# A Mamba-style block on one core: the last pass's y laid down in row order, gates read back in two parts, and Pool's share of a convolution halved

## The reference, cut to what matters

```python
xi, z = split(x @ in_proj_w.T)                       # 192 channels each
xi = silu(depthwise_conv3x3(xi) + conv_b)
x_hwwh = stack([rows(xi), columns(xi)])              # two orders of the pixels
xs = concat([x_hwwh, flip(x_hwwh)])                  # four directions
# per direction: delta = softplus(dt), B, C from projections of xs; then the scan
h = exp(delta * A) * h + (delta * u) * B             # along L, for 16 states
y = sum_n(h * C) + D * u
# the columns' y is turned back to row order, and the four are added
y = y_rows + y_rows_flipped + turn(y_columns) + turn(y_columns_flipped)
y = layer_norm(y, on_g, on_b)                        # over the 192 channels
y = y * silu(z)                                      # the gates
out = y @ out_proj_w.T                               # 96 channels
x1 = inp * skip_scale + out;  x2n = layer_norm(x1, ln2_g, ln2_b)
```

## Time and profile before

| | |
|---|---|
| median of 3 runs | 13864.06 us (13862.24 to 13864.12) |
| the profiled execution | 13858.02 us, span 13856.2 us |
| mean granted TensorE clock | 0.894 of full speed |
| busy, share of the span | PE 78%, DVE 85%, Pool 75%, ACT 50% |

### The profile page before, as it was taken

How to read it: one execution, slowest core, us unless ns; L and a number is a source line. 1 busy time by engine, 2 the same in 40 slices (tenths; PEclk the granted TensorE clock), 3 DMA queues, 4 the chain that set the end, 5 groups by cost and what they waited for, 6 DMA issues and landing times. The chain is left out here.

```text
span 13856.2 us, 95545 instructions
## 1 busy us (share of the span) xinstructions
PE 10835.5 (78%) x24854; PEld 4165.7 (30%) x24854; DVE 11827.1 (85%) x8429; ACT 6948.7 (50%) x10308; POOL 10323.1 (75%) x4469
## 2 busy tenths in 40 slices
PE   6777877778777787877877778787787777877778
PEld 2333323333233332333322333233332323323333
DVE  6999579995799957999579995799957999579995
ACT  4454455554545445555455454554544545545455
POOL 5999359993599925999259992699926999269992
PEclk8999889999899997999889998899988999989998
DMA  4677346773467734677346773477734677347772
GB/s 136 215 219 215 94 128 214 221 213 91 135 213 221 214 85 137 214 220 214 83 138 215 219 215 80 140 217 218 216 78 141 215 219 215 77 148 215 219 215 72
DMA packets 765007, 2408.50 MB, mean 174 GB/s; under 512 B 205712, under 2 KB 207760, under 8 KB 752976
## 3 DMA queue, kind: packets, MB, share of 16 engines
q1 hardware_dynamic: 764400, 2401.78, 58.8%
HBM read 2300.18 MB, written 67.11 MB: 171 GB/s over the span
## 5 line engine op out<-in xcount | busy, mean ns | idle before, releaser
L1225 POOL TENSOR_TENSOR state<-state,c_sb 128x1024 f32<-128x1024 f32 x3072 | 7179.5, 2358 | 450.6 <-ACT carry L1052 448.7
L988 PE MATMUL ps<-state,wt 128*128 128x512 f32 x12288 | 6310.4, 656 | 144.2 <-ACT ya L1046 108.8
L988 PEld LDWEIGHTS ps<-state,wt 128*128 128x128 f32 x12288 | 2547.5, 211 | 3015.4 <-issue 2454.3
L1184 DVE TENSOR_TENSOR_SCAN state<-decay,carry,ps 128x1024 f32<-128x1024 f32 x1440 | 3379.5, 2347 | 86.2 <-DVE ps L1171 36.6
L1052 ACT COPY carry<-state 128x1 f32<-128x1 f32 x3072 | 586.2, 191 | 4870.7 <-DVE state L1184 4860.8
L965 PE MATMUL ps<-parts,sel 114*128 114x512 bf16 (+1 forms) x3840 | 1282.7, 419 | 2127.0 <-DVE state L1184 2125.6
L1214 POOL TENSOR_TENSOR dbu<-b_sb,du 128x1024 f32<-128x1024 f32 x1152 | 2717.1, 2359 | 231.9 <-DVE du L1199 231.9
L1171 DVE TENSOR_TENSOR ps<-ps,du 128x1024 f32<-128x1024 f32 x1920 | 2323.5, 1210 | 0.9
L1094 ACT ACTIVATE decay<-delta,a_neg 128x1024 f32<-128x1024 f32 x1920 | 2195.3, 1144 | 6.2
L1184 DVE TENSOR_TENSOR_SCAN state<-ps,carry,dbu 128x1024 f32<-128x1024 f32 x864 | 2013.4, 2330 | 4.1 <-POOL dbu L1214 4.1
L965 PEld LDWEIGHTS ps<-parts,sel 114*128 114x128 bf16 (+1 forms) x3840 | 259.8, 100 | 3678.3 <-DVE state L1184 3426.1
(11 more groups left out here) (208 smaller groups left out, 10860.9 us busy)
## 6 DMA issues: line engine op xcount, KB each, us to landing
c_sb<-bc SPq DMA_DIRECT2D x2048, 512.0 KB, 4.3
c_sb<-bc SPq DMA_DIRECT2D x2048, 256.0 KB, 5.5
b_sb<-bc SPq DMA_DIRECT2D x768, 512.0 KB, 4.6
b_sb<-bc SPq DMA_DIRECT2D x768, 256.0 KB, 5.4
x_nat<-x SPq DMA_DIRECT2D x17, 1536.0 KB, 9.2
gates<-gate_a SPq DMA_DIRECT2D x8, 2048.0 KB, 6.8
gate_a<-gates SPq DMA_DIRECT2D x8, 2048.0 KB, 8.8
x_tok<-x SPq DMA_DIRECT2D x288, 48.0 KB, 1.8
```

Source lines behind the costliest of these rows:

```text
L988: mm = pe.matmul(py[:, q * CH:(q + 1) * CH], col("ident"), state[:, slot(g, n), q * CH:(q + 1) * CH], start=(n == 0), stop=False)
L1184: dve.tensor_tensor_scan(state[:, slot(g, n), way], rate, what, 0.0 if fresh else carry[:, n:n + 1], ALU.mult, ALU.add)\
L1225: pool.tensor_tensor(state[:, slot(g, n), :], state[:, slot(g, n), :], c_sb[:, n % CRING, :], ALU.mult).then_inc(S["weighted"], 1)
```

## The change

Four edits:

1. `prep_b`: Pool's part of the remainder's convolution is 8 image rows (512 elements per partition) instead of 16. DVE does 8 more rows (`OWN_ROWS`) in the upper half of `conv_acc`, in nine taps behind its second group of taps of the a part. ACT takes `conv_acc` out when both are done.
2. `scan`: in the last pass `take_y` writes a new tile `y5`, in two copies: partitions 0 to 63 as they are, and partitions 64 to 127, which hold columns, into row order, reading PSUM with a step of 64 elements.
3. `post_a`: with `y5` in one order, `fold` is one matmul with a matrix `fold_w` (two identities side by side, twice), and the mean is taken of `ya` and `y5` themselves. It no longer waits for the folded copy, but `fold` of the next chunk waits until this one is centred. Pool adds the squares of the remainder to those of the a part, so that the variance needs one matmul. ACT's gain and offset go into DVE's instructions (`scalar_tensor_tensor`). The lags of the stages are shorter by one.
4. `post_a`: the gates and gn come back in two parts, the first two chunks and the other six, each with its own semaphore; the weights of the later part share the second one.

```diff
-POOL_ROWS = HH // 2
+POOL_ROWS = HH // 4
+OWN_ROWS = HH // 4
+FIRST = 2
...
+                nc.vector.tensor_tensor(fold_w[:, 0:DR], low, up, ALU.add)
+                nc.vector.tensor_tensor(fold_w[:, DR:128], low, up, ALU.add)
...
+                    act.wait_ge(S["conv_r"], 18)
+                    ur_out(conv_acc[:, :], 0, POOL_ROWS + OWN_ROWS).then_inc(S["ur_ready"], 1)
...
+                    def r_tap(t, before=0):
+                        if before:
+                            acc, first, last = rc(conv_acc[:, CH:SC]), POOL_ROWS, POOL_ROWS + OWN_ROWS
+                        else:
+                            acc, first, last = rc(ps2[2][:, :]), POOL_ROWS + OWN_ROWS, HH
...
-                    for i in range(1, NCH // SLOTS):
-                        a_taps(i)
+                    a_taps(1)
+                    for t in range(9):
+                        r_tap(t, 9)
+                    a_taps(2)
+                    a_taps(3)
...
-                        act.copy(chunk(yr if T % 3 == 2 else ya, T, at), like(py[:, :], T)).then_inc(S["y_taken"], 1)
+                        if T == 5:
+                            act.copy(y5[0:DR, span(at * SC, SC)], py[0:DR, :])
+                            by_row = y5[DR:128, :].rearrange("p (h w) -> p h w", w=W)
+                            last = act.copy(by_row[:, :, span(at * (SC // H), SC // H)],
+                                            py[DR:128, :].rearrange("p (w h) -> p h w", h=H))
...
+                    for part, here in ((slice(0, FIRST * CH), "back_first"), (slice(FIRST * CH, L), "back_in")):
+                        sp.dma_start(gate_a2[:, part], gate_dram[0:DA, part]).then_inc(S[here], 16)
+                        sp.dma_start(gate_r2[:, part], gate_dram[DA:DI, part]).then_inc(S[here], 16)
+                        sp.dma_start(gn_2[:, part], gn_dram[:, part]).then_inc(S[here], 16)
...
                     def fold(j):
-                        turned = yr[:, :].rearrange("p (w h) -> p h w", h=H)[:, rows(j), :]
-                        wait_free(pe, S["yr_copied"], j)
-                        pe.matmul(bank["yr"], col("ident"), yr[:, sl(j)], start=True, stop=False)
-                        pe.matmul(rc(bank["yr"]), hi_, turned, start=False, stop=True).then_inc(S["yr_mm"], 1)
+                        wait_free(pe, S["on_centered"], j)
+                        pe.matmul(bank["yr"], fold_w[:, :], y5[:, sl(j)], start=True, stop=True)\
+                          .then_inc(S["yr_mm"], 1)
+                        pe.matmul(bank["on_mean"], col("ones_di"), ya[:, sl(j)], start=True, stop=False)
+                        pe.matmul(bank["on_mean"], col("ones_di"), y5[:, sl(j)], start=False, stop=True)\
+                          .then_inc(S["on_mean_mm"], 1)
+                    def var_192(j):
+                        pe.wait_ge(S["sq_added"], j + 1)
+                        wait_free(pe, S["on_log"], j)
+                        pe.matmul(bank["on_var"], col("ones_di"), sqa[:, sl(j)], start=True, stop=True)\
+                          .then_inc(S["on_var_mm"], 1)
...
+                    for j in range(NCH):
+                        pool.wait_ge(S["on_squared"], j + 1)
+                        pool.tensor_tensor(sqa[0:DR, sl(j)], sqa[0:DR, sl(j)], sqr[:, sl(j)], ALU.add)\
+                            .then_inc(S["sq_added"], 1)
...
+                        dve.scalar_tensor_tensor(ya[:, sl(j)], ya[:, sl(j)], col("on")[:, 0, 0:1], rs[:, sl(j)],
+                                                 ALU.mult, ALU.mult).then_inc(S["on_unit"], 1)
...
+                            dve.wait_ge(S["back_first"], 48)
+                        if j == FIRST:
+                            dve.wait_ge(S["back_in"], 64)
...
+                        dve.scalar_tensor_tensor(ya[:, sl(j)], ya[:, sl(j)], col("on")[:, 0, 1:2], gate_a2[:, sl(j)],
+                                                 ALU.add, ALU.mult)
...
-                    staggered((1, on_center), (3, on_unit), (3, gate), (4, skip),
+                    staggered((0, on_center), (2, on_unit), (2, gate), (3, skip),
```

More of the change, by code:

```diff
@@ L205, in build @@
     yr = big("yr", 5 * KB16)
+    y5 = big("y5", 0)
     KB4 = SC * 4
@@ L683, in tap_times @@
                         tap = pad_r[:, t // 3:t // 3 + POOL_ROWS, t % 3:t % 3 + W]
-                        pool.tensor_scalar(rc(conv_tap[:, t % 2, :] if t else conv_acc[:, :]), tap,
+                        pool.tensor_scalar(rc(conv_tap[:, t % 2, :] if t else conv_acc[:, 0:CH]), tap,
                                            col("conv_wr")[:, t:t + 1], None, ALU.mult).then_inc(S["conv_p"], 1)
@@ L694, in _ @@
                         pool.wait_ge(S["conv_p"], t + 1)
-                        pool.tensor_tensor(conv_acc[:, :], conv_acc[:, :], conv_tap[:, t % 2, :], ALU.add)\
+                        pool.tensor_tensor(conv_acc[:, 0:CH], conv_acc[:, 0:CH], conv_tap[:, t % 2, :], ALU.add)\
                             .then_inc(S["conv_sum"], 1)
@@ L810, in _ @@
                 def _(dve):
-                    def r_tap(t):
-                        acc = rc(ps2[2][:, :])
-                        tap = pad_r[:, POOL_ROWS + t // 3:HH + t // 3, t % 3:t % 3 + W]
+                    def r_tap(t, before=0):
[3 more added lines that the diff above has]
+                            acc, first, last = rc(ps2[2][:, :]), POOL_ROWS + OWN_ROWS, HH
+                        tap = pad_r[:, first + t // 3:last + t // 3, t % 3:t % 3 + W]
                         weight = col("conv_wr")[:, t:t + 1]
@@ L818, in r_tap @@
                         else:
-                            dve.wait_ge(S["conv_r"], t)
+                            dve.wait_ge(S["conv_r"], before + t)
                             dve.scalar_tensor_tensor(acc, tap, weight, acc, ALU.mult, ALU.add)\
@@ L1045, in take_y @@
                         act.wait_ge(S["y_summed"], g + 1)
-                        act.copy(chunk(yr if T % 3 == 2 else ya, T, at), like(py[:, :], T)).then_inc(S["y_taken"], 1)
+                        if T == 5:
[3 more added lines that the diff above has]
+                                            py[DR:128, :].rearrange("p (w h) -> p h w", h=H))
+                        else:
+                            last = act.copy(chunk(yr if T == 2 else ya, T, at), like(py[:, :], T))
+                        last.then_inc(S["y_taken"], 1)
                     def carry_on(T, g, n):
@@ L1400, in on_unit @@
                         dve.wait_ge(S["on_rsqrt"], j + 1)
[L1401 to L1403 removed]
+                        dve.scalar_tensor_tensor(ya[:, sl(j)], ya[:, sl(j)], col("on")[:, 0, 0:1], rs[:, sl(j)],
+                                                 ALU.mult, ALU.mult).then_inc(S["on_unit"], 1)
+                        dve.scalar_tensor_tensor(yrc[:, sl(j)], yrc[:, sl(j)], col("on", DR)[:, 1, 0:1],
+                                                 rs[0:DR, sl(j)], ALU.mult, ALU.mult).then_inc(S["on_unit"], 1)
                     def gate(j):
                         if j == 0:
[L1407 to L1411 removed]
+                            dve.wait_ge(S["back_first"], 48)
+                        if j == FIRST:
+                            dve.wait_ge(S["back_in"], 64)
+                        dve.wait_ge(S["on_unit"], 2 * j + 1)
+                        dve.scalar_tensor_tensor(ya[:, sl(j)], ya[:, sl(j)], col("on")[:, 0, 1:2], gate_a2[:, sl(j)],
+                                                 ALU.add, ALU.mult)
+                        dve.wait_ge(S["on_unit"], 2 * j + 2)
+                        dve.scalar_tensor_tensor(yrc[:, sl(j)], yrc[:, sl(j)], col("on", DR)[:, 1, 1:2],
+                                                 gate_r2[:, sl(j)], ALU.add, ALU.mult).then_inc(S["gated"], 1)
                     def skip(j):
```

69 lines of the change are left out of this document (21 added, 48 removed).

## The result

| | before | after |
|---|---|---|
| median | 13864.09 us (13862.24 to 13864.36, 4 runs) | 13703.12 us (13687.03 to 13704.50, 4 runs) |
| profiled execution, span | 13858.02, 13856.2 us | 13702.17, 13700.3 us |
| mean granted TensorE clock | 0.894 | 0.892 |

The ratio is 0.9882 (95% interval 0.9864 to 0.9899): 161 us faster, where 90 were forecast. 13703 lies inside the range (13690 to 13840), 71 us under the forecast and 5 us from the rival "the clock stays full", although the clock did not stay full.

The account below looks back on a forecast made before the run. VectorE was taken to bound the scan, TensorE the stage after it, and Pool to end the convolution before it. Per image 12.4 - 4.0 - 1.8 + 4.7 = 11.3 us, 90 for 8: 13774 us, range 13690 to 13840.

Parts of the forecast that it names:

- the clock stays full: Rival: PE's clock does not fall after the scan; 20.8 us gained per image, 13698 us; chance 0.16.
- the strided read: Scan's last pass: each second y copy, reading PSUM with a step, takes 1.92 us; 5.8 us lost per image.
- the half clock: Stage after the scan: idle PE drops to 1.2 GHz, taking 9.5 us per image from a gain of 14.2.
- the ring: Stage after the scan: the next fold waits through DVE, ACT, Pool and PE's variance; 8.0 us per chunk.
- the mechanism before the scan: Convolution before the scan: Pool ends sooner, DVE is next late, the transfers behind stay the same; 12.4 us gained per image.
- edit 4 at nothing: Stage after the scan: gates read back in two parts are hidden; cost 0, bounds -1 and 2 us.
- 4d - 1.9: Scan: us lost per image, with d the time of one second y copy; 5.8, ends 2.1 and 9.5.
- of which 1.7 for half clock in the tail stay: Stage after the scan: of its 90.4 us before, 1.7 us come from half clock at its end and remain.
- The ring is longer: Rival: after the scan, Pool's addition near 2.35 us or four slow rings; stage loses some 2 us, 13827 us; chance 0.10.
- Dear read: Rival: the copy reading PSUM with a step takes 3.84 us, 13.5 us lost per image, 13835 us; chance 0.10.
- slower: Rival: the copy reading PSUM with a step takes 5.6 times the contiguous one, 13892 us; chance 0.04.
- nothing from Pool: Rival: Pool's halved convolution instructions keep their length, so 0 gained before the scan, 13873 us; chance 0.05.

Follow-up runs that it names:

- the part alone: The kernel before with only Pool's convolution part cut to 8 image rows and DVE doing 8 more: 13766.67 us, ratio 0.9935.
- the two turned kernels: Changed kernel with the second `y5` copy writing SBUF with the step: 13723.81 us; changed kernel with the eight column-pass copies reading PSUM with the step: 13648.82 us.
- the filler kernel: Changed kernel with added matmuls that nobody reads, on PE before the first three variances (four, four, two): 13656.92 us, ratio 0.9857.
- a single reorder on one engine: Changed kernel with PE's fold and mean of a chunk ahead of the variance of the chunk before: 13645.96 us, ratio 0.9846.
- both together: Changed kernel with PE's fold ahead of the previous chunk's variance and ACT's copy of the folded remainder ahead of the root: 13584.18 us, ratio 0.9806.

## Why the prediction was right, and where not

The time lies inside the range, but the sum is not confirmed by that: three prices (the strided read, the half clock, the ring) were too dear, all in the same direction, and the range reached down to the case of the full clock.

**Right: the mechanism before the scan.** Pool's end, DVE as the next late one, and the transfer chain unchanged behind SP's release came as told; the part alone gave 90 us against 12.4 x 8 = 99. The missing 1 us per image is mostly DVE's wait for PE ahead of its first group of a taps. It is 0.95 us where the granted clock is 1.00 from the convolution's start, and 2.5 to 3.6 where it is 0.50 for the first 3 to 5 us of it (the second image: 2.55 us, and 0.78 in the window of the first 8 us). The latter are five images of eight, and their stage before the scan takes 97.3 to 99.6 us instead of 96.7. The kernel before had the same in four images, the third for one:

```profile
3567.58 5.26 DVE L833 SCALAR_TENSOR_TENSOR ps<-pad_a,conv_w,ps 128x1024 f32<-128x1024 f32 x4 [2.51 <-PE ps L711]
```

There it cost nothing, since Pool ended last; once DVE is last, it counts. What makes the clock low at that place in some images I did not test. The nine taps took 6.8 us (forecast 6.9). Pool's `tensor_scalar` took 1.56 us, not half of 2.84; its 7 us of slack covered that, as the prediction said it would.

**Right: edit 4 at nothing**, shown by the kernel without it.

**Mis-sized: the strided PSUM read.** The step was "I take 1.92, by the nearest row". It was the lower bound, 1.007 us. The row that was nearest in form had the step on the other memory, and that decides, as the two turned kernels show. With d = 1.0 the prediction's formula 4d - 1.9 gives 2.1, and 3.1 us were measured: it counts 0.72 in each of the two chunks (measured 1.07 and 1.06), -0.22 in the last one, where nothing can be gained (measured 0), and 0.88 at the end (measured 1.0). The net miss is 2.7 us per image, 21 us in all. The section "Memory Cachelines" of "Advanced Engine Details and Errata" in the Trainium skill says that a pattern that isn't contiguous in PSUM slows matmuls; for ACT's reads the trace shows no such price (1.007 against 1.002 us). Its remark on SBUF, that each access on another line costs, agrees with the 1.91 us.

**Mis-sized: the half clock.** The step was "I count two rings in full and parts around them, 9.5 us". The direction was right: PE idle, Pool named, clock down, then 1.00. But no ring was at half clock in full: with 3.5 us of PE's work at half clock it would take some 11.1 us, and the longest of the eight images took 10.5. The first windows show a granted clock of 0.79, a mean over parts at 1.2 and parts at 2.4 GHz. The first two rings there took 9.28 and 9.87 us against 7.58; by the filler kernel's images in which the clock never fell the whole is 5.7 us. A second term failed beside it, "of which 1.7 for half clock in the tail stay": in the tail of the changed kernel's stage the clock is 1.00 in all eight images (the window at 3280 in the second). The page "TensorE: Matmul & The Clock Gate" of the Trainium skill, section "What's actually happening", had the direction and not the size; what the prediction said of it, "its sum would be mine", would be off by as much.

**Mis-sized: the ring.** The steps were "PE: variance 1.05, fold 1.0, mean 2.1" and "the ring takes 8.0 us". Steady, it is 7.59. A matmul pair follows a pair of the same full rows after 0.86 us; the 1.05 that I used was read beside matmuls of 64 rows (L1265). So the variance is 0.96, the fold 0.86 and the mean 1.72 us, 0.6 less together, and a hand-over of 0.2 from PE to DVE that the sum lacked gives a part back. Seven rings at 0.41 less are 2.9 us, of which the second ring gives 0.6 back (see the rivals), so that the stage at full clock is 72.1 us (the filler kernel's) where the prediction had 74.5. With 3.8 for the half clock (9.5 less 5.7) and 1.7 for the tail this makes 7.9 us. The second image, against which the sum was made, took 0.7 longer than the mean of the eight before (90.4 against 89.7), which leaves 7.2; the stage came out 7.3 us better than forecast.

**The rivals.** "The clock stays full" gave nearly the right time, 13698, for a wrong reason: it kept the dear copy and the long ring. Judged by the time alone it would have won, and the windows refute it. "The ring is longer" named Pool's addition beside DVE: one of the eight per image did take 1.85 us, and made the second ring 0.6 us longer (8.18 us instead of 7.58 in the filler kernel, at full clock), but the others took 1.25 to 1.27. "Dear read", "slower" and "nothing from Pool" are refuted by L1063's 1007 ns and by the -11.4 us.

**What the prediction did not see** is that the ring could have been left out: the order of `fold` and variance on PE, and of the copy and the root on ACT, cost 14.3 us per image, more than the 12.0 that this stage gained by the change.

## What to carry to other kernels

When a change creates a ring between engines, write down what stands in it on each in-order engine, and move out what the ring doesn't need; a single reorder on one engine gives only up to the next ring (70.3 us), both together made the stage bound by PE (63.5 us), and in six of eight images the clock then stayed at 1.00 without any filler. When ACT turns data on its way out of PSUM, put the step on the PSUM side. Work that ended second before a change ends last behind it, and its own delays, which cost nothing, then count. A price borrowed from a row holds only if the row has the same memory on the same side and the same neighbours.

## What the runs showed of the hardware

- ACT reads fp32 from PSUM with a step of 256 bytes at the speed of a contiguous read: 1.005 us for 1024 elements on 128 partitions, 1.007 on 64. With the step on the SBUF side it is 1.91 to 1.92 us on either. DVE's product over SBUF and PSUM costs 1.92 us with the step in the SBUF operand that it reads, 1.94 with the step in what it writes and in PSUM, and 1.20 without.
- Matmul pairs of 512 fp32 columns on full rows start 0.86 us apart at full clock (3243.73 and 3244.59 above). Beside a pair of 64 rows it is 1.05, as PE's timeline of the kernel before has it:

```profile
3275.15 1.13 PE L1264 MATMUL ps<-ya,wt 128*128 128x512 f32 x2
3276.21 1.12 PE L1265 MATMUL ps<-yrc,wt 64*128 64x512 f32 x2
```

- A Pool addition and a DVE `scalar_tensor_tensor` that meet delay each other: 1.85 us instead of 1.25 and 1.75 instead of 0.74, in the two rows at 3224, and in each of the eight images. Beside the instruction that forms x1 (L1434), which has one operand in PSUM, the same addition takes 1.26. The "GPSIMD Engine Reference" of the Trainium skill, section "Specifications", says that Pool shares its SBUF interfaces with VectorE and names contention with DVE instructions of two SBUF inputs; this agrees.
- Adding idle-filling matmuls made the kernel 40 us faster, since PE's next work then ran at full clock.
- The same instructions in the same order meet either clock: at the start of this stage it was 0.50 in five of the changed kernel's eight images and 1.00 in three, behind the same idle time of 2.4 us on PE.
